# dt projected channel-major, segment sums in two fp32r passes, and the first context moved ahead, in a four-layer kernel

## The reference, cut to what matters

```python
weights = softmax(einsum('bci,bcj->bij', x, x))       # channel attention, 256 x 256 a batch
context = einsum('bij,bcj->bci', weights, x)
# then an MLP with 4-bit weights (gate, up, gelu, down; 2048 wide)
zxbcdt = u @ W_in.T                                   # state-space layer
dt = softplus(dt + dt_bias)                           # 4 heads
xBC = silu(causal depthwise conv of 4 taps)
A_dt = -exp(A_log) * dt
L = exp(segsum(A_dt))                                 # sums of A_dt between two tokens
Y = C B^T * L applied to x * dt, plus the state carried over, plus x * D
y = rmsnorm(Y * silu(z)) @ W_out.T
# then an MLP of 1024 with the two largest of each four kept
```

## Time and profile before

| | |
|---|---|
| median of 3 runs | 1367.37 us (1366.83 to 1368.35) |
| profiled execution, own time | 1377.32 us |
| its span | 1375.6 us |
| mean granted clock | 0.963 |
| PE busy | 1281.5 us (93%) |
| DVE, ACT, POOL busy | 912.1, 608.8, 464.7 us |

### The profile page before, as it was taken

The page is one execution under the profiler, slowest core; times in us unless marked ns, Lnnn a source line. Parts: engine busy times, 40 slices in busy tenths (PEclk is TensorE's granted clock), DMA queues, the critical chain, the costliest instruction groups (busy, mean ns, idle before and its releaser), DMA issues.

```text
span 1375.6 us, 20883 instructions
## 1 busy us (share of the span) xinstructions
PE 1281.5 (93%) x7224; PEld 1068.2 (78%) x7224; DVE 912.1 (66%) x1734; ACT 608.8 (44%) x1125; POOL 464.7 (34%) x568
## 2 busy tenths in 40 slices
PE   6699999999999999999899999999999799999994
PEld 6577888888888888888667767767767687888884
DVE  3486645453534444446588678678676799999997
ACT  3243323232323232334666666666664444444441
POOL 1244300000000000000354554453444566677775
PEclk9899999999999999999899999999999999999997
DMA  4122101000000001000000110010110101010000
GB/s 179 51 77 96 31 1 31 1 16 16 1 31 0 30 0 46 0 16 1 28 26 18 35 43 9 33 43 8 35 43 16 39 1 31 30 30 30 30 16 31
DMA packets 30404, 41.38 MB, mean 30 GB/s; under 512 B 2433, under 2 KB 22913, under 8 KB 30209
## 3 DMA queue, kind: packets, MB, share of 16 engines
q1 hardware_dynamic: 30336, 40.53, 9.0%
HBM read 27.94 MB, written 12.58 MB: 29 GB/s over the span
## 4 chain that ended last, share of the span: by engine, by line
PE 61%; DVE 22%; issue 9%; ACT 6%; POOL 1%; DVEq 1%; DMA 1%; ACTq 0%; POOLq 0%; SPq 0%; PEldq 0%
PE bank L44 18%; PE bank L46 17%; PE bank L45 17%; DVE acc L1153 3%; DVE dab L1313 2%; DVE beats L1297 2%; PE bank L1666 2%; PE bank L1672 2%; DVE dh L1279 2%; DVE rows_out L1346 1%; DVE mag L984 1%; DVE rank L1302 1%; PE bank L1655 1%; DVE st L1036 1%; PE bank L1634 1%
## 5 line engine op out<-in xcount | busy, mean ns | idle before, releaser
L1060 DVE TENSOR_TENSOR hb<-gl,bank 128x512 f32<-128x512 f32 x128 | 87.9, 687 | 200.1 <-PE bank L46 197.5
L670 ACT ACTIVATE hh<-hb 128x512 fp32r<-128x512 f32 x128 | 80.9, 632 | 182.2 <-DVE hb L1060 182.2
L709 ACT ACTIVATE gl<-bank 128x512 f32<-128x512 f32 x128 | 76.4, 597 | 181.8 <-PE bank L46 181.7
L1023 DVE TENSOR_TENSOR hl<-hb,hh 128x512 fp32r<-128x512 f32 x128 | 95.6, 747 | 84.5 <-ACT hh L670 84.5
L520 POOL TENSOR_TENSOR veb<-mvb,eps 128x4 f32<-128x4 f32 x8 | 1.8, 228 | 378.7 <-DVE mvb L1040 378.7
L44 PE MATMUL bank<-xt_l,w_h 128*128 128x512 f32 x256 | 103.8, 406 | 17.9 <-DVE xt_l L1023 15.6
L653 POOL TENSOR_TENSOR dhl<-dab,dhh 128x512 fp32r<-128x512 f32 x64 | 100.3, 1590 | 31.1 <-ACT dhh L670 31.1
L44 PE MATMUL bank<-at_l,w_hi_a 128*128 128x512 f32 x256 | 102.9, 402 | 1.3 <-DVE at_l L1023 1.0
L46 PE MATMUL bank<-xt_h,w_h 128*128 128x512 f32 x256 | 101.9, 398 | 0.0
L46 PE MATMUL bank<-at_h,w_hi_a 128*128 128x512 f32 x256 | 101.8, 398 | 0.0
L45 PE MATMUL bank<-xt_h,w_l 128*128 128x512 f32 x256 | 101.8, 398 | 0.0
(11 more groups left out here) (222 smaller groups left out, 3781.2 us busy)
## 6 DMA issues: line engine op xcount, KB each, us to landing
xg<-x_scratch SPq DMA_DIRECT2D x16, 512.0 KB, 3.9
xall<-in_x SPq DMA_DIRECT2D x8, 512.0 KB, 7.3
xg<-in_xt SPq DMA_DIRECT2D x8, 512.0 KB, 4.8
x_scratch<-rows_out SPq DMA_DIRECT2D x8, 512.0 KB, 3.2
x_scratch<-rows_out SPq DMA_DIRECT2D x16, 256.0 KB, 2.2
out<-rows_out SPq DMA_DIRECT2D x8, 512.0 KB, 3.2
wq<-in_codes SPq DMA_DIRECT2D x12, 256.0 KB, 2.6
sc<-in_scales SPq DMA_DIRECT2D x12, 256.0 KB, 2.9
```

The source lines that it names most:

```text
L670: return act.activation(dst, src, ACT.Copy)
L709: act.activation(gl[:, n % 2], ps_gate[n % 2][:], ACT.Gelu_apprx_tanh).then_inc(s_gelu, 1)
L1023: return dve.tensor_tensor(dst, src, hi.bitcast(F32), ALU.subtract)
L1060: dve.tensor_tensor(hb[:, n % 2], gl[:, n % 2], ps_up[n % 2][:], ALU.mult).then_inc(s_h, 1)
```

## The change

Three edits. At the begin, `context(0, 0)` on PE moves ahead of `scores` 4 and 5, and `x1_transpose(0)` ahead of scores 6 and 7; ACT and DVE take the same order, and piece 1's dequantisation moves behind the low parts that the first group's attention needs. dt is projected like the other channels, with the last 128 rows of W_in as the stationary operand and 512 tokens streaming; ACT copies the result to SBUF, PE transposes four blocks back, and DVE reads the last four columns of each. For the segment sums POOL splits the decay rates into an fp32r high part and the rest, makes two masked tensors, and PE adds two fp32r passes with an fp32r copy of `below` (whose entries are 0 and 1).

```diff
+            pool.wait_ge(s_const, 10)
+            pool.tensor_copy(below_r[:], below[:]).then_inc(s_const, 1)
...
             def masked_decay(n, t):
                 if t == 0:
                     pool.wait_ge(c_dtc, DT_STEPS * (n + 1))
                     pool.wait_ge(c_seg, NT * n)
-                pool.tensor_tensor(au[:, t], upto[:].unsqueeze(1).broadcast_to([P, HEADS, P]),
-                                   adt[:, t].unsqueeze(2).broadcast_to([P, HEADS, P]), ALU.mult).then_inc(c_au, 1)
+                    pool.tensor_tensor(adt_h[:], adt[:], ones[:, 0:NT * HEADS].rearrange("p (t h) -> p t h", h=HEADS),
+                                       ALU.mult).then_inc(c_ahl, 1)
+                    pool.wait_ge(c_ahl, 2 * n + 1)
+                    pool.tensor_tensor(adt_l[:], adt[:], adt_h[:].bitcast(F32), ALU.subtract).then_inc(c_ahl, 1)
+                    pool.wait_ge(c_ahl, 2 * n + 2)
+                mask = upto[:].unsqueeze(1).broadcast_to([P, HEADS, P])
+                pool.tensor_tensor(au_h[:, t], mask, adt_h[:, t].bitcast(F32).unsqueeze(2).broadcast_to([P, HEADS, P]),
+                                   ALU.mult).then_inc(c_au, 1)
+                pool.tensor_tensor(au_l[:, t], mask, adt_l[:, t].unsqueeze(2).broadcast_to([P, HEADS, P]),
+                                   ALU.mult).then_inc(c_au, 1)
...
             score_exp(0)
             x_hi(0)
+            softmax_hi(0)
             xs_hi(GPB)
-            softmax_hi(0)
             xs_hi(GPB + 1)
+            act.wait_ge(c_small, 96)
+            act.activation(a4[:], a4[:], ACT.Exp).then_inc(c_a4, 1)
             weights_hi(0)
             xs_hi(GPB + 2)
-            weights_hi(1)
             xs_hi(GPB + 3)
-            act.wait_ge(c_small, 96)
-            act.activation(a4[:], a4[:], ACT.Exp).then_inc(c_a4, 1)
             for k in range(KT):
                 a_hi(0, k)
+            weights_hi(1)
             score_exp(1)
...
+            def dt_keep(n):
+                act.wait_ge(c_dtp, n + 1)
+                copy(dt_rows[:], DT_LANE[:]).then_inc(c_dtk, 1)
...
                 if slot == 0 and part == 1:
+                    dt_keep(n)
                     dt_exp_ln(n, b)
...
             x_lo(0)
+            softmax_lo(0)
             xs_low(GPB)
-            softmax_lo(0)
             xs_low(GPB + 1)
             dequant(0)
             ln1_stats(0)
             xs_low(GPB + 2)
             ln1_apply(0)
-            dequant(1)
             xs_low(GPB + 3)
             for k in range(KT):
                 a_lo(0, k)
+            dequant(1)
             score_max(1)
...
-                dve.wait_ge(c_dtp, n + 1)
-                done(1, dve.tensor_tensor(d0[:], DT_LANE[:, 0:16].rearrange("p (t h) -> p t h", h=HEADS),
+                dve.wait_ge(c_dtt, n + 1)
+                done(1, dve.tensor_tensor(d0[:], DT_LANE[:, 0:NT * P].rearrange("p (t h) -> p t h", h=P)[:, :, P - HEADS:],
...
             softmax_transpose(0)
+            context(0, 0)
             scores(GPB)
             scores(GPB + 1)
-            context(0, 0)
+            x1_transpose(0)
             scores(GPB + 2)
             scores(GPB + 3)
-            x1_transpose(0)
...
-                pe.wait_ge(c_au, NT * n + t + 1)
-                pe.matmul(SEG_LANE[t][:], below[:], au[:, t].rearrange("p h l -> p (h l)"),
-                          start=True, stop=True).then_inc(c_seg, 1)
+                pe.wait_ge(c_au, 2 * (NT * n + t + 1))
+                pe.matmul(SEG_LANE[t][:], below_r[:], au_h[:, t].rearrange("p h l -> p (h l)"), start=True, stop=False)
+                pe.matmul(SEG_LANE[t][:], below_r[:], au_l[:, t].rearrange("p h l -> p (h l)"),
+                          start=False, stop=True).then_inc(c_seg, 1)
...
                     dt_proj(nxt)
                     in_proj_at(n, 0)
+                    dt_transpose(n)
                     in_proj_at(n, 1)
...
                 pe.wait_ge(c_xtl, KT * (n + 1))
+                cols = slice(D_IN - P, D_IN)
+                for k in range(KT):
+                    mm = exact3(pe, DT_LANE[:], win_h[:, k, cols], win_l[:, k, cols], xt_h[:, k], xt_l[:, k],
+                                start=k == 0, stop=k == KT - 1)
+                mm.then_inc(c_dtp, 1)
+
+            def dt_transpose(n):
+                pe.wait_ge(c_dtk, n + 1)
                 for t in range(NT):
-                    mm = tok_proj(DT_LANE[:, t * HEADS:(t + 1) * HEADS], t, slice(D_IN - HEADS, D_IN))
-                mm.then_inc(c_dtp, 1)
+                    mm = pe.transpose(DT_LANE[:, t * P:(t + 1) * P], dt_rows[:, t * P:(t + 1) * P],
+                                      wide_i[:, P:2 * P])
+                mm.then_inc(c_dtt, 1)
```

More of the change, by code:

```diff
@@ L86, in build @@
         below = sb("below", [P, P], F32)
+        below_r = sb("below_r", [P, P], F32R)
         ones = sb("ones", [P, D_STATE], F32)
@@ L185, in build @@
         d0 = cs("d0", [P, NT, HEADS])
+        dt_rows = cs("dt_rows", [P, TOK])
         dax = cs("dax", [P, NT * HEADS])
@@ L199, in build @@
         et = cs("et", [D_STATE, 2, NT, HEADS])
-        au = cs("au", [P, NT, HEADS, P])
+        adt_h = cs("adt_h", [P, NT, HEADS], F32R)
+        adt_l = cs("adt_l", [P, NT, HEADS])
+        au_h = cs("au_h", [P, NT, HEADS, P], F32R)
+        au_l = cs("au_l", [P, NT, HEADS, P], F32R)
         mm_ = cs("mm_", [P, 2, HEADS, P])
@@ L283, in build @@
         c_dtp = sem("dt_projected")
+        c_dtk = sem("dt_rows_kept")
+        c_dtt = sem("dt_token_major")
         c_dtc = sem("dt_steps_dve")
@@ L287, in build @@
         c_ea = sem("decays_ready")
+        c_ahl = sem("decay_rates_split")
         c_au = sem("masked_decay_ready")
@@ L904, in _ @@
             z_silu(0, 1)
+            dt_keep(0)
             dt_exp_ln(0, 0, mid=False)
@@ L993, in dequant @@
                                              ALU.mult, ALU.mult).then_inc(s_wf, 1)
-            dve.wait_ge(s_const, 10)
+            dve.wait_ge(s_const, 11)
             def xs_low(f):
@@ L1384, in _ @@
         def _(pe):
-            pe.wait_ge(s_const, 10)
+            pe.wait_ge(s_const, 11)
             def scores(f):
@@ L1697, in _ @@
             dt_proj((0, 0, 0))
+            dt_transpose(0)
             for t in range(NT):
```

## The result

The changed kernel is slower: 1385.38 us median (1384.05 to 1386.06, 4 runs) against 1367.86 us, ratio 1.0097 with a 95% interval of 1.0072 to 1.0121. The forecast was 1360.0.

A forecast was written before the change was run, and what follows sets the result against it. PE was seen waiting for DVE at the begin, for DVE and ACT alternately in the loop, with clock falls on top. 1377.3 - 11.0 + 4.3 - 0.7 = 1369.9, less 9.9 over the median, gave 1360.0; range 1350 to 1366.

The forecast's parts named there:

- begin: Before the first gelu: context ahead of scores 4 and 5 starts the first group earlier, -11.0 us (-13 to -5).
- first gelu to the loop, the prologue in it: Before the loop: POOL's eight masks and two splits make the segment sums late, +4.3 us (+3 to +6).
- seven steps of the loop: State-space loop: -0.2 - 1.2 + 0.8 + 0.5 = -0.1 a step, -0.7 us in all (-12 to +17).
- the wait for x1: At the begin: it likely makes one stretch of some 3.4 us at 1.2 GHz, costing 1.7 us.
- Rival C: Begin: gives only 5 us back, as piece 1's low part or what follows holds the up projection; 1366 us, chance 0.12.
- dt: Loop: convolution 5.2 us after dt's start, -0.2 a step; dense matmuls remove the clock's fall, -1.2 a step.
- +0.8 a step: Loop, chunk 3: wait for `ee` grows to about 2.4 us and lowers the clock in about four of five steps.
- +0.5: Loop, chunk 1: POOL's longer masks delay DVE's multiplication `L1260`, +0.5 us a step (0 to 1.0).
- Rival S: Loop: clock stays low for two stretches behind the decay sums' wait, +2.5 a step, +17.5; 1378 us, chance 0.04.
- Rival F: Loop: masks block DVE the full 1.04 us in chunks 1 and 2, +1.5 a step more; 1371 us, chance 0.05.

The follow-up runs named there:

- e2: Begin and dt edits on the kernel before, old segment sums kept: 1352.9 us, ratio 0.985.
- f3: The changed kernel with each pair of segment passes made twice, so PE stays busy longer: 1369.2 us, ratio 0.9986.
- f6: The changed kernel with POOL's low mask of tile 1 moved behind xd's multiplication in chunk 2: 1365.9 us, ratio 0.9961.
- g1: The changed kernel with the old order at the begin (dt and segment-sum edits only): 1387.4 us, ratio 1.0138.
- f7: The changed kernel with POOL's low mask of tile 1 moved later and the segment passes made twice: 1358.2 us, ratio 0.9896.
- f8: Begin and dt edits on the kernel before, old segment sums, plus seven unused matmuls a step in chunk 2's PE waits: 1346.6 us, ratio 0.9816.
- g4: The changed kernel plus nine unused matmuls in chunk 2's PE waits, single segment passes: 1356.9 us, ratio 0.9903.
- e1: The begin edit alone on the kernel before: 1361.8 us, ratio 0.991.
- e3: Begin and segment-sum edits on the kernel before, old dt kept: 1370.8 us, ratio 0.9992.
- g2: Begin and segment-sum edits on the kernel before, old dt, segment passes made twice: 1369.0 us, ratio 0.9982.

## Why the prediction was wrong

In the profiled executions, by the terms of the sum:

| term | forecast, us | measured, us |
|---|---|---|
| begin | -11.0 | -13.7 (first gelu) |
| first gelu to the loop, the prologue in it | +4.3 | +5.8 (606.3 to 612.1) |
| seven steps of the loop | -0.7 | +13.9 (354.0 to 367.9) |
| all behind them | 0 | +2.3 (351.5 to 353.8) |
| sum | -7.4 | +8.3 |
| profiled execution over its median, before less after | -9.9 | -0.2 |

The forecast took 9.9 us off at the end, as if the profiled execution of after would stand as far above its median as that of before. It stood 0.2 above, so of the 25.4 us between 1360.0 and 1385.4 this step makes 9.7 and the terms 15.7. In the runs of before the clock goes with the time, 0.971 at 1365.2 us and 0.963 at 1377.2, so most of those 9.9 us were further falls in one execution, and no run shows that a changed kernel would keep them. What makes the +2.3 behind the loop is open.

**Begin.** Right in mechanism, and 2.7 too small: the 3.4 us at 1.2 GHz that I expected from the wait for x1 did not come, the clock records show none between 31 and 54 us. Rival C is out.

**Prologue.** Eight masks from 647.72 to 655.84, POOL late before each sum, as forecast. The term is 1.5 short. Its own numbers (670.4 against 667.2) gave 3.2, and the further 1.1 was not worked out; 5.9 was measured, from dt's first matmul to the loop (17.2 us before, 23.1 after). The clock that "may stay low" did stay low: 0.50 over 17 us, where e2 has 6.8 us of it. In f3, where PE is busy between the masks, it rose earlier, and the way from dt's first matmul to the loop is 21.0 us instead of 23.1. The clock over that stretch of after:

```profile
645.00:662.00 17.00, 9.59 (x22) 6.40 (x23) 4.28 (x12) 6.89 (x11) 10.56 (x17) 0.50 0.10 32
```

**dt.** Right. The convolution starts 728.87 - 723.76 = 5.1 us after dt's first matmul (forecast 5.2), the transposes 2.9 behind it (forecast 2.8), and the edit on top of the begin is worth 8 to 9 us (forecast 9.8).

**The failed step is the one that priced the segment sums: "one of 2.4 should do it in about four of five steps, each 1.3 us in PE's own part ... +0.8 a step", beside "+0.5" for the block as DVE time alone.** The waits themselves were well forecast: 2.36 in chunk 3 (1.15 and 1.21), 0.67 for the block in chunk 1. Wrong was their price. The block was costed by its length on DVE, 0.5, and not by what it does to PE: it doubled PE's idle time in front of `g_transpose`, from 0.7 in e2 to 1.38, just ahead of the old wait of 1.57, and PE was then at 1.2 GHz for 6.8 us in five of seven steps and for 3.4 in the other two, half of each lost. One of the five, the first, has no blocked multiplication, so not every fall there is the block's. In chunk 3 the low clock lasted 6.8 and not 3.4 us in four steps. e2, which has the same dt and the old sums, has falls in chunk 2 in four steps, one of them of 6.8, and none in chunk 3. Waits of its PE in its seven steps:

```profile
PE bank L44 <- DVE acc L1162: 11.1, 7, 1.7
PE bank L1619 <- DVE rows_out L1222: 4.9, 7, 0.7
PE bank L1547 <- ACT ee L818: 4.0, 7, 0.9
PE bank L1561 <- DVE acc L1162: 2.3, 3, 0.8
```

Mending the two places one at a time (f6, f3) gave 13.0 and 11.9 us of the seven steps back, 1.9 and 1.7 a step, against 0.5 and 0.8 in the sum. These prices belong to the place where the loop of after starts in its pattern: g1, with the same loop, has 358.4 us and not 367.9 in its seven steps. Rival S named this mechanism and nearly this price, for chunk 3 alone, with a chance of 0.04; the argument against it, that the falls seen before had cost 1.6, took their size over from a kernel in which PE had no second idle time so near. Rival F's place did not come: the block is in chunk 1 alone in most steps, 0.69 or 1.17 in the others as before.

The Trainium skill, "TensorE: Matmul & The Clock Gate", "A second HAM failure mode: psum-queue depth-cycling", tells of short idle times between groups of matmuls that send the clock back and forth; the trace agrees, with no single wait of PE in the loop of after over 1.7 us and the clock at 0.91.

f7, with all three edits, one instruction moved and the waits of chunk 3 filled, runs in 1358.2, near the forecast. That is another kernel, and the forecast had taken 9.9 us off without ground, so the nearness is luck.

## What to carry to other kernels

Shortening PE's work in front of a wait for another engine saves nothing and thins PE out. When the clock has already fallen nearby in the profile, price each new wait with the clock behind it (here 0.67 us a step came to 1.9), above all where two waits come to stand close together, and take the price as uncertain: where the steps start in their pattern moved it by 9.5 us in seven steps. A test is cheap: matmuls into a free bank inside the wait. If the kernel gets faster with them, the clock was the cost, and they can stay until real work is found for the place. And before a difference from a trace is set against a median, look at how far that trace's execution stands from its own median. When an instruction is added on POOL, look at which DVE instruction with both inputs in SBUF it will now run beside: 0.6 us more or less in the queue decided it here.

## What the runs showed of the hardware that was not expected

The effects of two edits on the clock don't add: dt -9 us, sums +9, both +24. The same loop started 12.4 us later took 9.5 us less over seven steps, with the same sequence of step lengths entered at another place (g1). Unused matmuls of 0.233 us, 49 of them in seven steps (f8), made a kernel 6 us faster (5 by the ratios) and 63 (g4) made one 28.5 us faster. Five kernels with quite different falls (before, e1, e3, f3 and g2) settle at steps of 51.1 to 51.3 us late in the loop, although at full clock a step needs 48.0 to 48.7; this was seen, and not explained.
